# VectorE order in the second layer of a recurrent/attention kernel: the side scan's pieces directly behind the row maxima, or last in each slot

## What is computed

```python
xn = layernorm(x);  s = state_space_scan(xn);  g = silu(moe_8_experts_top2(xn));       x = x + s * g
xn = layernorm(x);  s = causal_attention(xn);  g = silu(latent_attention_moe(xn));     x = x + s * g

# the state-space scan of layer 0 (the "side scan" below)
dt = softplus(xn @ Wdt + bdt);  B, C = xn @ WB + bB, xn @ WC + bC          # 16 states per channel
h[t] = exp(dt[t] * A) * h[t-1] + (xn @ Wx + bx)[t] * dt[t] * B[t]
y[t] = sum over the 16 states of h[t] * C[t];   s = (y * sigmoid(xn @ Wz + bz)) @ Wout + bout
```

## The kernel before

| slot mod 24 | scan piece | what follows it before |
|---|---|---|
| 0 / 1 | weigh / add | - / result (L1956 to L1959), average (L1965) |
| 2 / 3 | enter (gate in 50, 146) / step | combine (L1850, L1854), recs / finish in 51, 147 |
| 4 / 5 | weigh / add | end0 (L1860 to L1870) / norm (L1879), take_heads |
| 6 / 7 | enter / step | heads (L1798), scale (L1885) / - |
| 8 / 9 | weigh / add | scale2, key (L1891 to L1899), recs / queries0 (L1782 to L1785) |
| 10 / 11 | enter (gate in 82) / step | - / finish in 83, router (L1902 to L951), take_heads |
| 12 / 13 | weigh / add | queries1 (L1782 to L1785) / - |
| 14 / 15 | enter / step | rank (L966 to L975), recs / hidden 0 (L1803) |
| 16 / 17 | weigh / add | hidden 1 to 3 / hidden 4, take_heads |
| 18 / 19 | enter (gate in 18, 114) / step | - / maxima of the plain attention (L1938) |
| 20 / 21 | weigh / add | finish in 20, 116, expert gating (L1943), recs / L1950 |
| 22 / 23 | enter / step | - / down (L1953), take_heads |

## Time and profile before

### The profile page before, as it was taken

One profiled execution on the slowest core, in us unless ns is written; L12 is line 12 of the kernel. 1 busy time (PEld: TensorE's weight loads), 2 busy tenths in 40 slices (PEclk: granted clock), 3 DMA queues, 4 the chain that ended last, 5 costly groups with the idle time before them and its releaser, 6 DMA issues.

```text
span 1265.0 us, 19206 instructions
## 1 busy us (share of the span) xinstructions
PE 1086.1 (86%) x6753; PEld 685.2 (54%) x6753; DVE 959.1 (76%) x1490; ACT 622.3 (49%) x1111; POOL 303.5 (24%) x371
## 2 busy tenths in 40 slices
PE   6669999999777888889888988998898888999897
PEld 6457877788433434444553554464454446446454
DVE  6847887988367876888788798888889988654424
ACT  3647758665322534346535553655554453363532
POOL 2075554551312200420320141032024021000000
PEclk9679999999886788899989988998998999999989
DMA  7567777775334243345225433542533530230010
GB/s 198 181 213 246 231 235 224 227 226 166 118 61 133 78 106 81 103 112 113 87 80 124 128 96 83 135 117 71 124 103 103 109 101 29 35 69 27 18 44 17
DMA packets 97069, 150.24 MB, mean 119 GB/s; under 512 B 26984, under 2 KB 55984, under 8 KB 96912
## 3 DMA queue, kind: packets, MB, share of 16 engines
q1 hardware_dynamic: 73840, 72.33, 22.6%
q0 software_dynamic: 22976, 76.43, 20.1%
q10 hardware_dynamic: 160, 0.26, 0.1%
HBM read 124.33 MB, written 11.54 MB: 107 GB/s over the span
## 4 chain that ended last, share of the span: by engine, by line
PE 36%; DVE 19%; issue 7%; ACT 6%; DMA 4%; SPq 1%; POOL 1%; DVEq 0%; ACTq 0%
PE bank L1245 8%; PE bank L1274 3%; DVE neg_max L1767 3%; PE bank L1334 3%; PE bank L1325 3%; DVE sc_state L298 2%; PE bank L1339 2%; ACT probs L1569 2%; DMA q_all<-turned_rows 2%; PE bank L1293 2%; PE bank L1251 2%; PE bank L1329 2%; PE bank L1253 1%; DVE sc_y L315 1%; PE bank L191 1%
## 5 line engine op out<-in xcount | busy, mean ns | idle before, releaser
L1569 ACT ACTIVATE probs<-bank 128x1024 f32<-128x1024 f32 (+1 forms) x192 | 169.1, 881 | 277.7 <-PE bank L1251 201.2
L1767 DVE TENSOR_REDUCE neg_max<-bank 128x2 f32<-128x1024 f32 (+3 forms) x256 | 203.0, 814 | 116.6 <-PE bank L1251 77.5
L1245 PE MATMUL bank<-q_all,kk 49*128 49x512 f32 (+3 forms) x1024 | 205.6, 501 | 51.1 <-ACT probs L1569 26.3
L212 POOL DMA_DIRECT2D sc_bc_wide<-scan_bc x128 | 73.0, 572 | 442.6 <-DVE sc_ub L291 243.8
L1245 PEld LDWEIGHTS bank<-q_all,kk 49*128 49x128 f32 x1024 | 87.3, 196 | 153.0 <-ACT probs L1569 55.2
L779 PE MATMUL bank<-xcol,wst 128*128 128x256 f32 x624 | 148.9, 382 | 0.6 <-ACT xcol L841 0.6
L298 DVE TENSOR_TENSOR_SCAN sc_state<-sc_a,sc_ub 128x1024 f32<-128x1024 f32 x64 | 145.9, 2280 | 0.0
L1293 PE MATMUL bank<-kr,q_all 48*128 48x512 f32 (+3 forms) x512 | 116.8, 491 | 33.2 <-DVE neg_max L1767 32.2
L900 POOL DMA_INDIRECT xrow<-sorted_in,token_of x78 | 102.1, 1309 | 118.7 <-PE bank L766 64.3
L779 PEld LDWEIGHTS bank<-xcol,wst 128*128 128x128 f32 x624 | 113.6, 192 | 13.4 <-issue 0.9
L1274 PE MATMUL bank<-probs,vaug 128*32 128x512 f32 (+3 forms) x1024 | 100.2, 490 | 0.0
(11 more groups left out here) (307 smaller groups left out, 1783.8 us busy)
## 6 DMA issues: line engine op xcount, KB each, us to landing
sc_bc_wide<-scan_bc POOLq DMA_DIRECT2D x128, 512.0 KB, 4.7
wst<-in_wexp SPq DMA_DIRECT2D x39, 512.0 KB, 3.6
q_all<-q_kind SPq DMA_DIRECT2D x94, 128.0 KB, 4.3
rec_wide<-head_recips SPq DMA_DIRECT2D x31, 256.0 KB
p_t<-gates_turned SPq DMA_DIRECT2D x14, 512.0 KB, 6.1
sorted_out<-xrow SPq DMA_DIRECT2D x7, 640.0 KB
rows_all<-in_x SPq DMA_DIRECT2D x8, 256.0 KB, 4.3
sorted_in<-rows_all SPq DMA_DIRECT2D x8, 256.0 KB, 5.6
```

What stands on the lines that cost most here:

```text
L1245: mm(bank[1][:, par, at:at + n], kk[rows, b % 2, kt * P:(kt + 1) * P], q_all[rows, quad // 2 % 3, pair, kt * P:L].bitcast(F32), start=(at ...
L1569: af(probs[:, slot % RING, :, 0:width], bank[1][:, :, 0:width], ACT.Exp, scale=0.125).then_inc(s["p_ready"], 1)
L1767: last = v.tensor_reduce(neg_max[:, quad % 2, pr:4:2, i], bank[0][:, :, at:at + (i + 1) * P], AX, ALU.max, negate=True)
```

## The change

All scan pieces of slots 0 and later (slots 0 to 146: the `weigh` and `add` of chunk 3 and all of chunks 4 to 39, and the five gates) leave their place behind the row maxima. They are issued at the end of DVE's slot, behind `finish` and all side work, and ahead only of the reciprocals (L1971) and `take_heads` (L1794). Slots before 0 keep the old order. `make_u` gets one more wait, since it may now stand closer to a reader of its tile. Nothing is computed differently and no other engine's list is touched.

```diff
@@ make_u
         dve.wait_ge(s["sc_dt"], b + 1)
+        if b >= 1:
+            dve.wait_ge(s["sc_ub"], NC * b)
@@ DVE's slot, behind reduce_maxima and end_rope
-                    if (at := chunk_due(slot, 0)) is not None and at != (SCANNED, 1):
+                    if (at := chunk_due(slot, 0)) is not None and slot < 0 and at != (SCANNED, 1):
                         scan.enter(dve, *at)
-                    if (at := chunk_due(slot, 1)) is not None and at != (SCANNED, 1):
+                    if (at := chunk_due(slot, 1)) is not None and slot < 0 and at != (SCANNED, 1):
                         scan.step(dve, *at)
-                    if (at := chunk_due(slot, 2)) is not None:
+                    if (at := chunk_due(slot, 2)) is not None and slot < 0:
...
-                    if (at := chunk_due(slot, 3)) is not None and at[1] >= 1:
+                    if (at := chunk_due(slot, 3)) is not None and slot < 0 and at[1] >= 1:
                         scan.add(dve, *at)
-                    if (at := scan_due(slot, "gate")) is not None:
+                    if (at := scan_due(slot, "gate")) is not None and slot < 0:
                         scan.gate(dve, at[0])
@@ DVE's slot, behind average1
+                    if (at := chunk_due(slot, 0)) is not None and slot >= 0:
+                        scan.enter(dve, *at)
+                    if (at := chunk_due(slot, 1)) is not None and slot >= 0:
+                        scan.step(dve, *at)
+                    if (at := chunk_due(slot, 2)) is not None and slot >= 0:
+                        scan.weigh(dve, *at)
+                    if (at := chunk_due(slot, 3)) is not None and slot >= 0 and at[1] >= 1:
+                        scan.add(dve, *at)
+                    if (at := scan_due(slot, "gate")) is not None and slot >= 0:
+                        scan.gate(dve, at[0])
                     if (quad := quad_due(slot, INVERT)) is not None and quad < QUADS - 1:
```

## The result

| | before | after |
|---|---|---|
| median of 4 runs each | 1263.0 us | 1288.49 us (1285.44 to 1292.46) |
| ratio, 95% interval | | 1.0207 [1.0166, 1.0249] |
| profiled execution / its span | 1266.92 / 1265.0 | 1285.44 / 1283.6 |
| mean granted TensorE clock | 0.917 | 0.911 |
| DVE busy | 959.1 us | 959.5 us |

A forecast was written before the change was run, and what follows sets the result against it. Neither PE nor DVE full, pace set slot by slot; gates +3.9, clock +2.4, A -1.3, B -2.6, C and D 0, E +1.1, F -1.5 make +2.0 us: 1266.5 against the median 1264.53, range 1257 to 1275.

The forecast's parts named there:

- slots 11 and 12: Router and second queries: `prob` earlier releases ACT and the latents' DMA, second queries start about 1.4 earlier, `weigh` behind adds 1.1.
- the net of slots 8 to 13: Key, router and second queries in periods B to F: later key and `weigh` against earlier queries, net -0.3 us each.
- the clock behind the gates: PE's longer waits in slots 51 and 147 bring the low clock: +1.6 and, half taken, +0.8; together +2.4 us.
- Period A: Slot 8 +1.1, `weigh` +1.1, POOL's load leaving the query DMAs' stretch -1.5, slots 19 to 23 -2.0: sum -1.3 us.
- Period B: Slots 19 to 23: PE's 3.65 us wait for ACT 2.0 shorter, high clock behind it -1.6, +1.0 returned: -2.6 us.
- the gates: Slots 50 and 146: gate behind the combine delays PE's `project_out`, 1.96 us each, +3.9; with the clock +2.4 more.
- slot 8: `weigh` now follows the key instead of running while PE makes it: +1.1 us in A, +0.7 in B to F.
- hidden 0: Slots 15 to 18: DVE idles some 2 us for PE's matmul, slot 16's maxima 1.3 late, covered by slot 19: cost 0.
- the rival for slower: Slots 15 to 18 of B to F: hidden 0's wait not covered, 1.3 us five times, 1273.2 us; chance 0.25.
- slots 19 to 24 of C: Plain attention's reductions and ACT 2.0 earlier, about 1.0 reaching slot 23, returned by `step` behind the down addition: 0.
- Slots 0 to 7: They hold 24 slots' heaviest DVE work without idle time; order inside a slot changes nothing for the next maxima.
- my sign for the slower rival: Periods C and D longer by 1 us or more would show the prediction wrong and point to the slower rival.

The follow-up runs named there:

- 5: Changed kernel with slots 8 to 13's pieces back behind the row maxima, except `step` of slot 11, still last: 1268.29 us, ratio 1.0033 to the kernel before.
- 6: Changed kernel with POOL's B-rows load of slot 11 held until the first six query DMAs landed: 1267.21 us, ratio 1.0021 to the kernel before.
- Experiment 7: Kernel before the change with only POOL's load of slot 11 held until the first six query DMAs landed: 1264.1 us, ratio 0.9989.
- 3: Changed kernel with the pieces of slots 14 to 17 of each period back behind the row maxima: 1285.5 us, ratio 1.0178 to the kernel before.
- experiment 2: Changed kernel with the pieces of slots 8 to 13 of each period back behind the row maxima: 1267.76 us, ratio 1.0032 to the kernel before.
- 8: Changed kernel with only the pieces of slots 18 to 21 last, all others and the gates in front: 1261.84 us, ratio 0.9964 to the kernel before.
- 4: Changed kernel with POOL's B-rows load of every chunk moved behind the C rows' load: 1307.24 us, ratio 1.0347 to the kernel before.

## Why the prediction was wrong

**The failed step** is the one on slots 11 and 12: "So the second queries start about 1.4 earlier", with the net of slots 8 to 13 put at -0.3 in B to F. Its first half held: `prob` came earlier, and ACT's wait fell from 4.89 to 2.71. Its second half took the DMAs behind ACT's copy to land earlier by what they were issued earlier. They don't, since POOL's load of 512 KB was in flight (5, 6): in period C the second queries start 9.0 us after slot 11's maxima, before 9.1. With `weigh` still to come behind them, slot 13 lost 0.8 on average where it should have gained. Over B to F slots 9, 13 and 15 cost 11.2 us, where the prediction had -1.5 in its text and nothing in its sum, which leaves the five times -0.3 out. I had seen such a load and its effect in period A, at 461.16, and had not asked in B to F which transfers the earlier issue would meet. The Trainium skill (DMA: Bandwidth & Descriptors, "Issuing engines are not separate DMA queues") says that transfers issued by different engines interleave on the same 16 DMA engines; experiments 5 and 6 agree (the last query DMA takes 5.9 us from issue to landing beside the load and 3.7 without it), and that rule should have been weighed at this step.

**A term that was missing** is the clock behind slot 13: PE's wait for the maxima grew from 2.04 to 4.68 us, and the granted clock of the 8 us behind it fell from 0.79 to 0.62. I had priced the clock behind the gates alone.

By periods, from slot 8 to slot 24, in us:

| | A | B | C | D | E | F | together |
|---|---|---|---|---|---|---|---|
| forecast | -1.3 | -2.6 | 0 | 0 | +0.4 | -1.5 | -5.0 |
| by the traces | +3.9 | +3.3 | +2.9 | +0.3 | +0.9 | +2.2 | +13.5 |

**Period A.** The C rows' load left the stretch as forecast, but gave back only 0.4 of the 1.5: the second queries start 9.0 us after slot 11's maxima, before 9.3. Experiment 7 shows which load it was, the B rows' one, for held back it gives 1.83. The largest part is the clock. PE waited for the maxima's rows of slot 18 about as long before as after, but behind the wait the granted clock was 1.00 before and 0.51 after (6 us from the wait's end on), and the same matmuls took 1.13 and 2.08. Before, then after:

```profile
485.76 1.13 PE L1245 MATMUL bank<-q_all,kk 49*128 49x512 f32 x4 [2.96 <-DMA q_all<-turned_rows]
```
```profile
489.62 2.08 PE L1247 MATMUL bank<-q_all,kk 49*128 49x512 f32 x4 [3.16 <-DMA q_all<-turned_rows]
```

So the length of a wait alone does not price it, and why the clock fell here stays open. The -2.0 of slots 19 to 24 that I expected came (2.2 at slot 21), but only took back part of that.

**Period B** should have lost PE's low clock in slot 46 (-1.6, with -2.6 for slots 19 to 24). The wait of the earlier trace rows fell from 3.65 to 2.87 only, the matmuls behind it stayed at the low level (4.56, before 3.98), and slot 24 came 0.1 later, counted from slot 18:

```profile
619.80 0.37 PE L1306 MATMUL bank<-c_ident,neg_max 128*16 128x128 f32 x1 [2.87 <-ACT p_t L1690]
619.96 4.56 PE L1336 MATMUL bank<-c_wd,hm 128*128 128x128 f32 x20
```

**Right** were:

- the gates: 6.3 forecast, 7.2 in the traces, 8.2 timed alone. The waits of 3.7 and 2.6 us came as said, and the clock behind them; too low was the half taken for it in slot 147 (0.8, where 3.58 less the 1.96 of the order leaves 1.6);
- slot 8: 1.1 in A and 0.7 in B to F forecast, 0.85 in A and 0.72 to 1.11 in the others found, at slot 9;
- hidden 0, whose wait costs nothing (3). So the rival for slower, though on the right side, had the wrong mechanism and place;
- slots 19 to 24 of C, where the gain of ACT is given back at slot 24 by `step` behind the down addition. `step` of slot 23 left in front keeps it: slot 72 loses 1.04 in experiment 2 and nothing in 8.

**Smaller misses.** Slots 0 to 7 were put at nothing, but in the changed kernel's trace the combines of slots 2 and 26 wait for their gather (1.23 and 1.14 us), while the one of slot 122, for which I had +0.7, does not. In the trace of experiment 3, whose order is the same there, neither slot 3 nor slot 27 loses anything, so these 2.6 us depend on more than the order. The prediction's opening also gave slot 71 to DVE, while the earlier trace rows has its maxima waiting 2.82 us for PE, and the slower rival's five times 1.3 are 6.5, not 6.7.

Period C grew by 2.87 and D by 0.3, so my sign for the slower rival (both by 1 or more) came for one of them and would have named the wrong cause. The mean clock moved by 0.006, less than the 0.01 at which I said the clock would explain the result by itself.

## What to carry to other kernels

When a change lets a transfer be issued earlier, list what the DMA engines carry at the new time, from whatever queue: an early issue into a busy stretch can land at the same time as before, as it did here. If it still pays to go early, hold back the big transfer that is not due, with a wait on a semaphore. An engine's list that is paced by semaphores alone does not stay in the slot in which its program puts it (4). And an order that is worse as a whole can hold parts that gain: five of the 24 slots, with one load held back, made this kernel 1.8% faster than the kernel before.

## What was not expected of the hardware

A wait of PE can be paid a second time behind it, but its length does not say how much. In slot 61 the same six matmuls took 4.15 us after a wait of 4.68, 3.69 after 2.04 and 2.84 after 1.09. At this place of periods B to F in all kernels here, they took 2.84 us after every wait up to 1.1 us and 2.84 or 2.96 after those of 1.5 to 1.9, but anything from 2.84 to 4.26 after waits of 2.0 to 4.7.

The last of the six query DMAs of 128 KB, in period C, took 3.7 us from issue to landing with the load held back, and 5.7 and 5.9 beside it. With a delay of 0.9 to 2.0 us for it in five of the six periods, and what followed from that, the one load cost the changed kernel 21 us.
